# Two attention layers on one core: projections on 64-row tiles, weighted sums on four 32-column tiles, whole-array work gathered once per step

## The chip, the cores and the metric
The kernel runs on one core of a Trainium2 chip. The metric is the device time of one execution, in microseconds. The engines are named as the profile names them: PE is the matrix engine (TensorE), DVE the vector engine, ACT the scalar engine, POOL is GpSimd, SP issues the DMA transfers.

## The reference
Four layers run one after the other over 8 batches of 256 rows of 160 numbers, all in 32-bit floats: a narrow cross-attention with 20 heads of 8 (l0), a self-attention with 20 heads of 64 (a1), a cross-attention with 20 heads of 64 over a context of 512 rows of 256 (a2), and a gated feed-forward layer (ff). a1 and a2 are what the change rewrites:

```python
n = layer_norm(x, g, b)                       # x: 8 x 256 x 160
q = n @ wq                                    # wq: 160 x 1280, 20 heads of 64
k, v = src @ wk, src @ wv                     # a1: src = n; a2: src = context, 8 x 512 x 256
attn = softmax(q @ k.T / 8)                   # for each head
x = x + (attn @ v) @ wo + bo                  # heads joined to 1280; wo: 1280 x 160
```

## The kernel before
`attention_layer` (line 213) builds a1 and, with `cross` true, a2. Numbers that feed the softmax are split in a high part, rounded to the fast matmul type (fp32r), and a low part, the rest; a product is high by high, low by high and high by low. So a projection of n (160 rows) contracts 3 x 160 = 480 rows: `N_TERMS` (line 35) lays them out as three pieces of 128 rows and one of 96. The context's 256 rows give six pieces of 128 (`CTX_TERMS`, line 36).

The work goes in steps of two head pairs, that is four heads, 256 of the 1280 columns; 5 steps make a batch, 40 a layer. Each engine has its own program `step(d)`, unrolled over all steps, and the programs meet in semaphores. The steps are pipelined: step d projects for d, scores for d-1, computes the turned scores (keys on partitions) and exponentials for d-2, and the weighted sums for d-3 and d-2. A step has 2 slots in a1 and 4 in a2.

On PE (line 485), in this order: in each slot `score` (line 347, two heads side by side as 64-row tiles, for the row maxima), `turned_scores` (line 362, again 64-row tiles, 16 matmuls of 256 columns), then in some slots whole-array work, `keys` (402), `values` (418), `queries` (389), `output` (449) and the transposes `turn_max` (460), and in some the `weighted_sums` (432), which put the two heads of a pair in two 64-column tiles and are FP32: such a matmul is two instructions. The sums of the probabilities come from GpSimd's adds over the key tiles (`key_sums`, line 717, adds of 128x512) and a matmul with ones of 64 columns.

DVE takes the maxima (`maximum`, 620; one buffer `pscore`, so the next score waits for the last maximum), the low parts (`low_queries`, `low_keys`), reciprocal and product (`normalise`, 633), the layer norm (`dve_stats`, `dve_xhat`, `dve_n32`, lines 148 to 196) and adds the output. ACT takes the exponentials (`exp`, 535; one buffer `pst`), the high parts, the copy of the values and of the turned maxima. The queries, the keys and the values have a PSUM buffer each (`pa`, `pb`, `py`). The weights are split before the first step, on DVE and GpSimd (`Weights.low`, line 90).

## Time and profile before
| what | value |
|---|---|
| time, median of 3 runs | 1908.17 us (1907.72 to 1909.85) |
| the profiled execution: time, span | 1908.41 us, 1906.6 us |
| PE busy | 1742.8 us, 91% |
| DVE busy | 1325.7 us, 70% |
| ACT busy | 916.6 us, 48% |
| POOL busy | 443.8 us, 23% |
| mean granted clock of PE | 0.972 |
| HBM | 14 GB/s over the span |

The span runs from the first to the last instruction; the time has 1.8 us around it. Durations of matmuls overlap, since they are pipelined: what one costs is read from start to start. In a timeline row the columns are start, duration of the merged run, engine, line, operation, output and inputs, shape and count; in brackets stands how long the engine had been idle and who released it.

### The profile page before, as it was taken

What the parts mean: (1) busy time and instruction counts of PE and PEld (TensorE: products, weight loads), DVE (VectorE), ACT (ScalarE), POOL (GpSimd) and SP (SyncE); (2) the same over time, 40 slices, a digit from 0 to 9 for tenths busy, and PEclk for the clock granted to TensorE, in tenths of its full rate; (3) what the DMA queues carried; (4) which work ended last, traced back from release to release, by engine and by line L of the source; (5) the groups of instructions that cost most, each with busy time, mean ns of one, the idle gap of its engine ahead of it and who ended that gap; (6) DMA issues with size and microseconds to landing.
All of it is one profiled execution on the core that took longest, in us unless ns stands there. A gap on an engine that the chain in (4) does not pass through costs nothing. (4 is left out here: it accounts for less than half of the span.)

```text
span 1906.6 us, 36445 instructions
## 1 busy us (share of the span) xinstructions
PE 1742.8 (91%) x14528; PEld 1359.1 (71%) x14528; DVE 1325.7 (70%) x2210; ACT 916.6 (48%) x1636; POOL 443.8 (23%) x360
## 2 busy tenths in 40 slices
PE   5999989999959999999976999999999999999768
PEld 4667666666547777777755777777777777778568
DVE  5877877788668877888756666666656666665456
ACT  5878767778634343343323443434433434343223
POOL 1000000000022222222222443434343434343400
PEclk9999989999979999999987999999999999999979
DMA  6000000000030000000001000000000000000010
GB/s 195 17 18 1 18 19 18 1 18 1 1 101 1 1 2 1 2 1 2 1 7 37 12 1 13 1 12 1 12 1 12 1 12 1 1 2 1 1 44 21
DMA packets 11056, 29.23 MB, mean 15 GB/s; under 512 B 1872, under 2 KB 4944, under 8 KB 10896
## 3 DMA queue, kind: packets, MB, share of 16 engines
q1 hardware_dynamic: 10896, 26.94, 4.4%
q8 instruction: 119, 1.95, 0.4%
q14 instruction: 41, 0.34, 0.1%
HBM read 25.63 MB, written 1.31 MB: 14 GB/s over the span
## 5 line engine op out<-in xcount | busy, mean ns | idle before, releaser
L638 DVE RECIPROCAL a_recip<-a_pv 128x256 f32<-128x256 f32 x160 | 280.3, 1752 | 68.9 <-PE a_pv L446 68.2
L726 POOL TENSOR_TENSOR a_half_sum<-raw_weights 128x512 f32<-128x512 f32 x160 | 204.8, 1280 | 447.1 <-ACT raw_weights L541 447.1
L1101 DVE TENSOR_REDUCE l_negmax<-l_pscore 128x1 f32<-128x77 f32 (+1 forms) x640 | 233.2, 413 | 74.4 <-PE l_pscore L878 70.0
L541 ACT ACTIVATE raw_weights<-a_pst 128x1024 f32<-128x1024 f32 x160 | 164.1, 1026 | 246.3 <-PE a_pst L384 246.3
L627 DVE TENSOR_REDUCE a_negmax<-a_pscore 128x2 f32<-128x1024 f32 x160 | 195.5, 1222 | 97.1 <-PE a_pscore L358 96.1
L1018 ACT ACTIVATE l_probs<-l_pst 128x512 f32<-128x512 f32 x320 | 184.4, 598 | 75.3 <-PE l_pst L890 74.3
L541 ACT ACTIVATE a_probs<-a_pst 128x1024 f32<-128x1024 f32 x80 | 82.0, 1025 | 230.2 <-PE a_pst L384 230.2
L733 POOL TENSOR_TENSOR a_key_sum<-a_probs 128x512 f32<-128x512 f32 x80 | 102.1, 1276 | 309.8 <-ACT a_probs L541 309.8
L442 PE MATMUL a_pv<-raw_weights,a_v 128*64 128x256 f32 x1280 | 157.0, 388 | 2.6 <-DVE raw_weights L640 2.6
L878 PE MATMUL l_pscore<-l_k,l_qm 128*128 128x512 f32 x320 | 147.4, 461 | 11.5 <-DVE l_negmax L1101 6.0
L644 DVE TENSOR_TENSOR a_ql<-a_pa,a_qh 128x512 fp32r<-128x512 f32 x80 | 54.9, 686 | 146.2 <-ACT a_qh L547 146.1
L414 PE MATMUL a_pb<-a_ct,a_wk 128*128 128x512 f32 x480 | 133.9, 415 | 7.6 <-DVE a_ct L609 6.6
L375 PE MATMUL a_pst<-a_qh,a_kh 64*128 64x256 f32 x960 | 136.4, 280 | 3.7 <-ACT raw_weights L541 2.9
L381 PE MATMUL a_pst<-a_ql,a_kh 64*128 64x256 f32 x960 | 136.1, 279 | 0.0
L378 PE MATMUL a_pst<-a_qh,a_kl 64*128 64x256 f32 x960 | 135.8, 279 | 0.0
L384 PE MATMUL a_pst<-a_neg_t,a_sel 64*128 64x256 f32 x960 | 135.2, 278 | 0.0
L890 PE MATMUL l_pst<-l_qm,l_k 128*128 128x256 f32 x640 | 131.0, 287 | 4.0 <-ACT l_probs L1018 3.3
L428 PE MATMUL a_py<-a_wv,a_ct 128*128 128x256 f32 x960 | 131.6, 287 | 0.0
L890 PEld LDWEIGHTS l_pst<-l_qm,l_k 128*128 128x128 f32 x640 | 115.9, 192 | 21.7 <-issue 5.0
L428 PEld LDWEIGHTS a_py<-a_wv,a_ct 128*128 128x128 f32 x960 | 122.6, 190 | 8.9 <-issue 0.2
L145 POOL MEMSET a_ln_half<- 128x2 f32 x2 | 0.2, 99 | 546.0 <-POOLq L774 528.6
L358 PE MATMUL a_pscore<-a_kh,a_qh 64*128 64x256 f32 (+1 forms) x640 | 120.5, 414 | 4.6 <-DVE a_negmax L627 4.3
(156 smaller groups left out, 3534.9 us busy)
## 6 DMA issues: line engine op xcount, KB each, us to landing
l_ct<-in_ctx_t SPq DMA_DIRECT2D x8, 512.0 KB, 3.8
a_ct<-in_ctx_t SPq DMA_DIRECT2D x8, 512.0 KB, 3.6
l_x<-in_x_t SPq DMA_DIRECT2D x8, 256.0 KB, 2.8
raw_weights<-in_a_wk SPq DMA_DIRECT2D x3, 640.0 KB, 8.8
raw_weights<-in_a_wv SPq DMA_DIRECT2D x3, 640.0 KB, 10.9
a_wo<-in_a_wo SPq DMA_DIRECT2D x2, 800.0 KB, 5.2
xs<-in_x SPq DMA_DIRECT2D x8, 160.0 KB, 3.9
raw_weights<-in_a_wq SPq DMA_DIRECT2D x2, 640.0 KB, 5.1
```

Of the source, the lines that this page charges most:

```text
L375: mm(pst[:, h, j * SQ:(j + 1) * SQ], kh[own[h], buf, i, kt], qh[own[h], buf, i, :], start=True, stop=False)
L381: mm(pst[:, h, j * SQ:(j + 1) * SQ], kh[own[h], buf, i, kt], ql[own[h], buf, i, :], start=False, stop=False)
L428: last = mm(py[:, j * 256:(j + 1) * 256], acts[0:rows, xs_, kt * P:(kt + 1) * P], wv[0:rows, ws, 2 * u * P:2 * u * P + 256], start=k == 0, ...
L442: mm(pv[own[h], 0:SQ], v[:, kt, c0:c0 + D1], probs[:, par, h, kt, :], start=kt == 0, stop=kt == KT - 1)
L541: nc.scalar.activation(probs[:, g % 2, :, 2 * n:2 * n + 2, :], pst[:].rearrange("p h (k q) -> p h k q", k=2), ACT.Exp, scale=SCALE).then_i ...
L627: nc.vector.tensor_reduce(to, pscore[:], AX.X, ALU.max, negate=True).then_inc(max_done, 1)
L638: nc.vector.reciprocal(recip[:], pv[:, SQ:2 * SQ]).then_inc(recip_done, 1)
L726: nc.gpsimd.tensor_tensor(half_sum[:, n], probs[:, par, :, 2 * n, :], probs[:, par, :, 2 * n + 1, :], ALU.add).then_inc(half_done, 1)
L878: mm(pscore[:, i % 2, :], qm[:, buf, j, qt * P:(qt + 1) * P], k4[:, buf, :], start=True, stop=True).then_inc(score_ready, 1)
L890: last = mm(pst[:, n % 2, i * SQ:(i + 1) * SQ], k4[:, buf, kt * P:(kt + 1) * P], qm[:, buf, j, :], start=True, stop=True)
L1018: nc.scalar.activation(probs[:, par, j, 2 * kb:2 * kb + 2, :], pst[:, n % 2, :].rearrange("p (k q) -> p k q", k=2), ACT.Exp, scale=SCALE). ...
L1101: last = nc.vector.tensor_reduce(negmax[:, par, qt, j, s:s + 1], pscore[:, i % 2, keys], AX.X, ALU.max, negate=True)
```

## The change
`attention_layer` is replaced by `self_attention_layer` and `cross_attention_layer`, and the layer norm of both by `PairedNorm`.
- Queries and keys of n are projected on two 64-row tiles, one for each head pair. For that the normalised input is laid out with its 64-row halves doubled and its last 32 rows four times (12 pieces on DVE instead of 6, 6 transposes instead of 4, 3 gain steps of 256 instead of 2, splits of 768 elements), and eight pieces of 64 rows (`N_ROWS`) replace the four. The keys of the context go the same way (12 pieces of 64 rows for each pair, 512 columns wide). The values of a1 are on 64-row tiles too; those of a2 stay on the whole array.
- The weighted sums of both pairs of a step are made together, on four 32-column tiles, in two passes (x) for the two halves of a head's 64 numbers, and the ones have 32 columns. A step has one reciprocal and two products. Pairs and halves are ordered so on the host, in the weights.
- Order on PE: scores, turned scores and projections in the slots, then output, weighted sums, transposes and (a2) values once, at the step's end. The output of a batch is one block of 40 instructions.
- Queries, keys and values share one two-bank buffer, `pj`; the turned maxima are put in `pscore`, the turned norm in `pst`, the output in `px`, which also takes half of the weighted sums. In a2 the probabilities have one buffer and the context comes in three transfers a batch, doubled. GpSimd adds 128x1024 once a step in a1, and six times 128x512 in a2; its reciprocal root stands ahead of the key sums. The pipeline is one step shorter.

The core of the diff: the norm, then a1 (PE, DVE, GpSimd), then a2 (PE, DVE, GpSimd), where the removed lines are left out for a2.

```diff
+    def dve_xhat(self, dve, m):
+        nc = self.nc
+        dve.wait_ge(self.rstd_ready, m + 1)
+        for qt in range(QT):
+            scalars = (self.mv[:, qt, 0:1], self.rstd[:, qt:qt + 1])
+            for k in range(2):
+                nc.vector.tensor_scalar(self.xhat[:, qt, 0:2, k * D1:(k + 1) * D1],
+                                        self.xs[:, m, qt, 0:P].rearrange("p (c d) -> p c d", c=2),
+                                        *scalars, ALU.subtract, ALU.mult)
+            for k in range(4):
+                last = nc.vector.tensor_scalar(self.xhat[:, qt, 2, k * REST:(k + 1) * REST],
+                                               self.xs[:, m, qt, P:C], *scalars, ALU.subtract, ALU.mult)
+        last.then_inc(self.xhat_ready, 1)
+
+        dve.wait_ge(self.xhat_ready, m + 1)
+        nc.vector.tensor_tensor(self.xs[:, m], self.xs[:, m], self.rows, ALU.add).then_inc(self.biased, 1)
...
+    def pe_transpose(self, pe, m):
+        pe.wait_ge(self.xhat_ready, m + 1)
+        for g in range(3):
+            for qt in range(QT):
+                last = self.nc.tensor.transpose(self.turned(g)[:, qt * P:(qt + 1) * P], self.xhat[:, qt, g, :],
+                                                self.ident)
+        last.then_inc(self.t_ready, 1)
...
+
+
+
+N_ROWS = [(0, 0, 0), (1, 0, 1), (2, 0, 0), (3, 0, 1), (0, 1, 0), (1, 1, 1), (4, 0, 2), (4, 1, 2)]
+
+C_ROWS = [(0, 0, s) for s in range(4)] + [(1, 0, s) for s in range(4)] + [(0, 1, s) for s in range(4)]
+
+C_FULL = [(hw, hc, s) for hw, hc in ((0, 0), (1, 0), (0, 1)) for s in range(2)]
+OWN = [slice(h * D1, (h + 1) * D1) for h in range(2)]
+STEPS1 = PAIRS // 2
...
+            def queries_keys(d):
+                b, u = divmod(d, STEPS)
+                if u == 0:
+                    pe.wait_ge(ln.n_ready, b + 1)
+                wait(pe, v_copied, d)
+                for which, w in enumerate((wq, wk)):
+                    for k, (ws, hl, s) in enumerate(N_ROWS):
+                        for t in range(2):
+                            last = mm(pj[:, t, which * SQ:(which + 1) * SQ], w[OWN[t], ws, u * P:(u + 1) * P],
+                                      nts[b % 2][OWN[t], hl, s, :], start=k == 0, stop=k == len(N_ROWS) - 1)
+                last.then_inc(qk_ready, 1)
+
+            def values(d):
+                b, u = divmod(d, STEPS)
+                pe.wait_ge(qk_split, d + 1)
+                for k, (ws, hl, s) in enumerate(N_ROWS):
+                    for t in range(KT):
+                        last = mm(pj[:, t, 0:STEP_COLS], nts[b % 2][OWN[t], hl, s, t * P:(t + 1) * P],
+                                  wv[OWN[t], ws, u * STEP_COLS:(u + 1) * STEP_COLS],
+                                  start=k == 0, stop=k == len(N_ROWS) - 1)
+                last.then_inc(v_ready, 1)
+
+            def weighted_sums(e):
+
+                wait(pe, ot_ready, e)
+                pe.wait_ge(v_copied, e + 1)
+                pe.wait_ge(exp_done, 2 * e + 2)
+                if output_at(e + 3) is not None:
+                    pe.wait_ge(y_taken, output_at(e + 3) + 1)
+                for x in range(2):
+                    for kt in range(KT):
+                        for t in range(4):
+                            mm((pv, px)[x][t * 32:(t + 1) * 32, 0:SQ],
+                               v[:, e % RING, kt, t * D1 + x * 32:t * D1 + (x + 1) * 32], probs[:, e % 2, t, kt, :],
+                               start=kt == 0, stop=kt == KT - 1)
+                pe.wait_ge(sum_ready, e + 1)
+                for t in range(4):
+                    last = mm(pv[t * 32:(t + 1) * 32, SQ:2 * SQ], ones[:], key_sum[:, e % 2, t, :], start=True, stop=True)
...
+            def step(d):
+                for i in range(2):
+                    if here(d - 1):
+                        score(d - 1, i)
+                    if here(d - 2):
+                        turned_scores(d - 2, i)
+                    if i == 0 and here(d):
+                        queries_keys(d)
+                if output_at(d) is not None:
+                    output(output_at(d))
+                if here(d - 3):
+                    weighted_sums(d - 3)
+                if here(d - 1):
+                    turn_max(d - 1)
+                if next_norm(d, LN_TURN):
+                    turn_norm(d)
+                if here(d):
+                    if d == 0:
+                        pe.wait_ge(wv_done, 2)
+                    values(d)
+
+            ln.pe_transpose(pe, 0)
+            pe.wait_ge(ones_set, 1)
+            pe.wait_ge(wo_in, 16)
+            pe.wait_ge(wq_done, 1)
+            pe.wait_ge(wk_done, 1)
+            for d in range(LAST):
...
+                dve.wait_ge(qk_hi, d + 1)
+                subtract(qkl[:, d % RING], pj[:].rearrange("p i (w q) -> p i w q", w=2),
+                         qkh[:, d % RING].bitcast(FP32)).then_inc(qk_split, 1)
...
+            def step(d):
+                for i in range(2):
+                    if here(d - 1):
+                        maximum(d - 1, i)
+                if here(d):
+                    low_queries_keys(d)
+                if next_norm(d, LN_STATS):
+                    ln.dve_stats(dve, next_norm(d, LN_STATS))
+                if next_norm(d, LN_XHAT):
+                    ln.dve_xhat(dve, next_norm(d, LN_XHAT))
+                if next_norm(d, LN_TURN):
+                    ln.dve_n32(dve, next_norm(d, LN_TURN))
+                if next_norm(d, LN_SPLIT):
+                    b = next_norm(d, LN_SPLIT)
+                    ln.dve_lo(dve, b, nts[b % 2])
+                if output_at(d) is not None:
+                    add_output(output_at(d))
+                if here(d - 3):
...
+            def key_sums(e):
+
+                wait(pool, pv_done, e - 1)
+                pool.wait_ge(exp_done, 2 * e + 2)
+                nc.gpsimd.tensor_tensor(key_sum[:, e % 2], probs[:, e % 2, :, 0, :], probs[:, e % 2, :, 1, :],
+                                        ALU.add).then_inc(sum_ready, 1)
...
+                wait(pe, v_copied, d)
+                for k, (ws, hl, s) in enumerate(N_ROWS):
+                    for t in range(2):
+                        last = mm(pj[:, t, 0:SQ], wq[OWN[t], ws, u * P:(u + 1) * P], nt[OWN[t], hl, s, :],
+                                  start=k == 0, stop=k == len(N_ROWS) - 1)
...
+            def keys(d, part):
                 b, u = divmod(d, STEPS)
+                if part == 0:
+                    if u == 0:
+                        pe.wait_ge(c_ready, b + 1)
+                    pe.wait_ge(q_split, d + 1)
+                half = len(C_ROWS) // 2
+                for k in range(part * half, (part + 1) * half):
+                    hw, hc, s = C_ROWS[k]
+                    for t in range(2):
+                        last = mm(pj[:, t, :], wk[OWN[t], hw, s, u * P:(u + 1) * P], cts[b % 2][OWN[t], hc, s, :],
+                                  start=k == 0, stop=k == len(C_ROWS) - 1)
+                if part == 1:
+                    last.then_inc(k_ready, 1)
+
+            def values(d):
                 b, u = divmod(d, STEPS)
+                pe.wait_ge(k_split, d + 1)
+                for kt in range(KT):
+                    for k, (hw, hc, s) in enumerate(C_FULL):
+                        last = mm(pj[:, kt // 2, (kt % 2) * STEP_COLS:(kt % 2 + 1) * STEP_COLS],
+                                  cts[b % 2][:, hc, 2 * s, kt * P:(kt + 1) * P],
+                                  wv[:, hw, s, u * STEP_COLS:(u + 1) * STEP_COLS],
+                                  start=k == 0, stop=k == len(C_FULL) - 1)
                 last.then_inc(v_ready, 1)
...
+            def weighted_sums(e):
+
+                wait(pe, ot_ready, e)
+                pe.wait_ge(v_copied, e + 1)
+                for n in range(2):
+                    pe.wait_ge(exp_done, SLOTS * e + 2 * n + 2)
+                    for x in range(2):
+                        if n == 0 and x == 1 and output_at(e + 2) is not None:
+                            pe.wait_ge(y_taken, output_at(e + 2) + 1)
+                        for kt in (2 * n, 2 * n + 1):
+                            for t in range(4):
+                                mm((pv, px)[x][t * 32:(t + 1) * 32, 0:SQ],
+                                   v[:, e % 2, kt, t * D1 + x * 32:t * D1 + (x + 1) * 32], probs[:, t, kt, :],
+                                   start=kt == 0, stop=kt == KT - 1)
+                pe.wait_ge(sum_ready, 2 * e + 2)
+                for t in range(4):
+                    last = mm(pv[t * 32:(t + 1) * 32, SQ:2 * SQ], ones[:], key_sum[:, t, :], start=True, stop=True)
...
+                    if here(d) and s == 0:
+                        queries(d)
+                    if here(d) and s in (1, 2):
+                        if d == 0 and s == 1:
+                            pe.wait_ge(wk_done, 1)
+                        keys(d, s - 1)
+                if output_at(d) is not None:
+                    output(output_at(d))
+                if here(d - 2):
+                    weighted_sums(d - 2)
+                if here(d - 1):
+                    turn_max(d - 1)
+                if next_norm(d, LN_TURN):
+                    turn_norm(d)
+                if here(d):
+                    if d == 0:
+                        pe.wait_ge(wv_done, 1)
+                    values(d)
+            pe.wait_ge(wq_done, 1)
...
             def step(d):
                 for s in range(SLOTS):
                     if here(d - 1):
                         maximum(d - 1, s)
+                    if s == 0:
+                        if here(d):
                             low_queries(d)
+                        if next_norm(d, LN_SPLIT):
+                            ln.dve_lo(dve, next_norm(d, LN_SPLIT), nt)
+                    if s == 1 and next_norm(d, LN_STATS):
+                        ln.dve_stats(dve, next_norm(d, LN_STATS))
+                    if s == 1 and next_norm(d, LN_XHAT):
+                        ln.dve_xhat(dve, next_norm(d, LN_XHAT))
+                    if s == 2 and next_norm(d, CTX_SPLIT):
+                        low_context(next_norm(d, CTX_SPLIT))
+                if output_at(d) is not None:
+                    add_output(output_at(d))
+                if here(d):
+                    low_keys(d)
+                if next_norm(d, LN_TURN):
...
+            def key_sums(e):
+
+                add = nc.gpsimd.tensor_tensor
+                wait(pool, pv_done, e)
+                for i in range(2):
+                    two = slice(2 * i, 2 * i + 2)
                     pool.wait_ge(exp_done, SLOTS * e + i + 1)
+                    add(key_sum[:, two], probs[:, two, 0, :], probs[:, two, 1, :], ALU.add).then_inc(part_sum, 1)
+                for i in range(2):
+                    two = slice(2 * i, 2 * i + 2)
+                    pool.wait_ge(part_sum, 4 * e + 2 + i)
+                    pool.wait_ge(exp_done, SLOTS * e + i + 3)
+                    add(key_sum[:, two], key_sum[:, two], probs[:, two, 2, :], ALU.add).then_inc(part_sum, 1)
+                    pool.wait_ge(part_sum, 4 * e + 3 + i)
+                    add(key_sum[:, two], key_sum[:, two], probs[:, two, 3, :], ALU.add).then_inc(sum_ready, 1)
 
             ln.pool_setup(pool)
...
+                if next_norm(d, LN_STATS):
                     ln.pool_rstd(pool, next_norm(d, LN_STATS))
+                if here(d - 2):
+                    key_sums(d - 2)
```

## Rows read from the trace of the kernel before
**Rows 1.** Busy by window, self and cross: length, PE, PEld, DVE, ACT, POOL; clock, DMA.
```profile
556.53:964.00 407.47, 399.80 (x3751) 318.62 (x3750) 330.63 (x436) 164.48 (x247) 101.90 (x83) 1.00 0.02 7
1025.39:1771.58 746.19, 727.59 (x6347) 573.73 (x6347) 472.99 (x562) 297.65 (x408) 296.43 (x235) 1.00 0.02 5
```

**Rows 2.** PE timeline of a cross step (instructions of weight loads left out).
```profile
1422.06 1.66 PE L414 MATMUL a_pb<-a_ct,a_wk 128*128 128x512 f32 x6
1423.56 1.58 PE L428 MATMUL a_py<-a_wv,a_ct 128*128 128x256 f32 x12
1425.07 0.50 PE L358 MATMUL a_pscore<-a_kh,a_qh 64*128 64x512 f32 x2
1425.41 0.28 PE L375 MATMUL a_pst<-a_qh,a_kh 64*128 64x256 f32 x2
...
1426.24 0.28 PE L384 MATMUL a_pst<-a_neg_t,a_sel 64*128 64x256 f32 x2
1426.45 1.95 PE L442 MATMUL a_pv<-raw_weights,a_v 128*64 128x256 f32 x16
1428.23 0.60 PE L446 MATMUL a_pv<-a_key_sum,a_ones 128*64 128x256 f32 x4
1428.76 1.21 PE L398 MATMUL a_pa<-a_nt,a_wq 128*128 128x256 f32 x8
...
1435.76 2.88 PE L456 MATMUL a_py<-a_wo,raw_weights 128*128 128x160 f32 x20
```

**Rows 3.** PE timeline: first scores of two neighbouring self and cross steps.
```profile
696.93 0.39 PE L358 MATMUL a_pscore<-a_kh,a_qh 64*128 64x256 f32 x2
...
706.31 0.39 PE L358 MATMUL a_pscore<-a_kh,a_qh 64*128 64x256 f32 x2
...
1384.21 0.49 PE L358 MATMUL a_pscore<-a_kh,a_qh 64*128 64x512 f32 x2
...
1401.97 0.50 PE L358 MATMUL a_pscore<-a_kh,a_qh 64*128 64x512 f32 x2
```

**Rows 4.** PE timeline in the first layer, four 32-column tiles, and the next instruction.
```profile
301.25 0.64 PE L938 MATMUL l_pv<-l_probs,l_v 128*32 128x256 f32 x8
301.81 0.48 PE L972 MATMUL l_pd<-l_sums,l_pick 128*128 128x256 f32 x1
```

**Rows 5.** Groups by form: busy us, mean ns, idle before and its releaser.
```profile
L638 DVE RECIPROCAL a_recip<-a_pv 128x256 f32<-128x256 f32 x160 | 280.3, 1752 | 68.9 <-PE a_pv L446 68.2
...
L627 DVE TENSOR_REDUCE a_negmax<-a_pscore 128x2 f32<-128x1024 f32 x160 | 195.5, 1222 | 97.1 <-PE a_pscore L358 96.1
...
L644 DVE TENSOR_TENSOR a_ql<-a_pa,a_qh 128x512 fp32r<-128x512 f32 x80 | 54.9, 686 | 146.2 <-ACT a_qh L547 146.1
...
L640 DVE TENSOR_TENSOR raw_weights<-a_pv,a_recip 128x256 f32<-128x256 f32 x80 | 34.0, 424 | 2.7
...
L541 ACT ACTIVATE raw_weights<-a_pst 128x1024 f32<-128x1024 f32 x160 | 164.1, 1026 | 246.3 <-PE a_pst L384 246.3
...
L547 ACT ACTIVATE a_qh<-a_pa 128x512 fp32r<-128x512 f32 x80 | 47.8, 598 | 95.6 <-PE a_pa L398 93.1
```

**Rows 6.** DVE and GpSimd timeline at the norm: a self, then a cross step.
```profile
714.61 0.50 DVE L173 TENSOR_SCALAR a_ln_xhat<-xs,a_ln_mv,a_ln_rstd 128x32 f32<-128x32 f32 x2
715.02 0.36 DVE L171 TENSOR_SCALAR a_ln_xhat<-xs,a_ln_mv,a_ln_rstd 128x160 f32<-128x160 f32 x1
...
715.83 0.49 DVE L178 TENSOR_TENSOR xs<-xs,a_bo_rows 128x320 f32<-128x320 f32 x1
...
1533.23 1.57 DVE L173 TENSOR_SCALAR a_ln_xhat<-xs,a_ln_mv,a_ln_rstd 128x32 f32<-128x32 f32 x2
...
1533.25 1.30 POOL L726 TENSOR_TENSOR a_half_sum<-raw_weights 128x512 f32<-128x512 f32 x1 [1.56 <-ACT raw_weights L541]
...
1534.84 1.44 DVE L178 TENSOR_TENSOR xs<-xs,a_bo_rows 128x320 f32<-128x320 f32 x1
```

**Rows 7.** PE timeline: the first keys of the cross layer.
```profile
1016.33 1.19 PE L414 MATMUL a_pb<-a_ct,a_wk 128*128 128x512 f32 x2 [6.63 <-DVE a_ct L609]
```

826 lines of the change are left out of this document (460 added, 366 removed).

## The prediction
> **What bounds the kernel now.** The shares of the page (the table above) name the matrix engine (PE), but they are a mean over four layers, of which the diff leaves the first and the last alone. So I asked the busy times by stage, from the first score matmul of each rewritten layer to the first of its last step: PE is busy 98% of 407 us in self-attention and 97.5% of 746 us in cross-attention, at full clock, with the vector engine (DVE) at 81% and 63% [rows 1]. So both layers are PE-bound, and the order of PE's own work sets the pace. The PE timeline shows what a step consists of [rows 2]. The reader is to look at start-to-start distances there, since durations overlap: a regular self step is 706.31 - 696.93 = 9.38 us, a cross step 1401.97 - 1384.21 = 17.76 us [rows 3].
>
> **What the edits are worth on PE.** Start-to-start prices [rows 2]: a pair of 64-row matmuls of 256 columns 0.118 us (1425.41 to 1426.24 is seven), a whole-array matmul of 256 columns the same 0.118 (12 between 1423.56 and 1425.07, less the change of shape), of 512 columns 0.23 (six in 1.50, less the change), and two 64-column FP32 instructions side by side 0.216 (eight such groups 1426.45 to 1428.23, less 0.05).
> - Projections. Before, two pairs' queries take 8 whole-array matmuls (four row pieces, the last with 96 rows); after, 8 pairs of 64-row matmuls: 0.94 us each way. The same holds for the self keys and values. Cross keys: 12 of 512 columns against 12 pairs, 2.8 us each way (only single pairs of 512 are shown; they lie between 0.216 and 0.23, at most 0.2 us a step). So the tiling itself gives nothing.
> - Weighted sums. Four 32-column tiles replace two 64-column ones, over twice the passes: 8 groups of 0.216 in self, 16 in cross, as before. Only the sums with ones halve, from 4 groups to 2: -0.43 us a step. Four tiles abreast are seen in the first layer: 8 instructions in 0.56 us with a change of shape in it, so two groups of about 0.22 [rows 4].
> - Changes of shape. Between two kinds of tiles the next start is late by about 0.1 us, and the first item costs 0.1 more: 1425.07 to 1425.41 is 0.34 for a pair worth 0.23, and 1428.23 to 1428.76 is 0.53 for two groups of 0.216. I take 0.20 for a change, 0.13 for one into the column tiles. Before, a self step has 6 and a cross step 10; after, each has 3 (4 with the output). That is -0.5 and -1.3 us.
> - The max transposes, the output (20 instructions in 2.72 us, so 5.44 a batch [rows 2]), scores and turned scores cost the same.
>
> Self step: two slots of 0.235 + 0.94, 1.88 for queries and keys, 0.09 + 1.78 + 0.53 weighted, 0.37 turn, 1.05 values = 8.05. Nothing late is longer: DVE has two maxima of 1.22, one split of 1024 (0.686 for 512 and 0.424 for 256 elements give 1.21), one reciprocal of 1.75 instead of two, two products of 0.42, in all about 6.3 us [rows 5]. -1.33 us a step.
>
> Cross step: PE's sum is 15.95, but two chains now end later. The projections share one buffer, so keys wait until the queries are out. A hand-over from PE takes the 0.28 us of the last matmul and up to 0.1 more. The first turned scores end at 1.43 us after the step's start, the exponential (1.03) at 2.5, then come the high part on the scalar engine (ACT, 0.6) and the low part on DVE (0.69) [rows 5]: keys start at 3.83, where PE was ready at about 3.4. With that the last exponential ends at 10.15; GpSimd then has two chained adds of 1.3 for the second pair [rows 6], so the sums stand at 12.95 where PE is ready at 12.5. Ones, turn and values end at 16.93. -0.83 us a step.
> Over the 39 steps between first and last score: -52 us and -32 us.
>
> **What the special steps take back.** A batch has steps with norm, output or splits. Before, they cost 407.5 - 39 x 9.38 = 41.7 us in self, plus 4.4 by which the first steps are short, so 46; in cross 53.6 + 7.5 = 61 [rows 1, 3]. After, for each of seven batches:
> - The normalised input. Its 6 pieces and the bias add become 12 and the add, 3.1 us of DVE at the 0.21 us from piece to piece of the smaller ones (two between 714.61 and 715.02), some more for the larger. DVE instructions that read and write SBUF alone wait out a GpSimd add: two pieces worth 0.50 took 1.57 and an add worth 0.49 took 1.44 while GpSimd was adding [rows 6]. In cross, max 1 ends at 4.9, and what is queued behind the pieces is max 2, for which score 3 waits. Free of GpSimd, score 3 starts at 9.2 instead of 7.7: 1.5 us. With GpSimd's adds at 5.0 to 6.2 and 7.8 to 10.3 it is 12.8: 5.1. I take 4.7, near the upper end, since the rows show the blocking. In self the one add of 1024 (2.6 us) starts just ahead of the pieces; the normalisation and then the next step's first max are queued behind: 1.9 to 4.0, taken 3.8.
> - The output in one block: 5.64 each, in self 0.7 more until the sum in the shared bank is taken. In cross that block covers the 0.4 us wait of the sums.
> - The transposed norm: 6 transposes instead of 4, 1.05 us; in self its three gain steps (0.45 apart) stand ahead of the normalisation and cost another 1.4.
> - Cross alone: the split of the norm delays max 1 by 0.9; and GpSimd's reciprocal root stands ahead of the key sums in its queue, waits for the statistics that follow max 1 on DVE (6.0), and six adds of 1.3 then end at 14.6: 1.65. The context split (2048 elements, 2.3 us of DVE, 2 of ACT) and its three loads lie beside the output.
> Sum: self 7 x (3.8 + 2.4 + 6.4) = 88, cross 7 x (9.9 + 1.05 + 0.9 + 1.65) = 94.5. Against before: +42 and +33.5, and +2.4 because the first steps, already short, save less.
>
> **Ends of the layers.** DVE splits more at the start, and GpSimd's split of 2560 elements (about 6 us at the rate of its adds) holds DVE up. In self the first projection stays where it was, but queries, split and values then follow one another: first score +3. In cross the keys start at about 1022 instead of 1016.3 [rows 7] and values wait for their split: first score +7.6. The pipeline is one step shorter, and a drained step has one reciprocal: -4.6 and -4.3. Net +1.7.
>
> **Sum.** -52 - 32 + 42 + 33.5 + 2.4 + 1.7 = -4.4 us. The profiled execution took 1908.4 us with a span of 1906.6, 0.2 above the median of 1908.2; so **1904 us**. 0.2%, about what a measurement of this kernel can tell from no change, is 4 us.
>
> **Rivals.**
> - **DVE is not held up** (faster). If the norm's pieces slip between GpSimd's adds, the stalls fall to 1.5 and 1.9: -22 - 13, 1868 us. For it: the same pieces in a self step run free, the add in 0.49 [rows 6]. Against it: this time GpSimd's adds are timed onto them by the exponentials.
> - **Four abreast does not stream** (slower). Four tiles need a weight load and a matmul every 54 ns; the fastest long stream in the trace, the paired 64-row matmuls, has one per 59 ns [rows 2], and the first layer shows four abreast only in bursts of 8 [rows 4]. At 59 the group takes 0.235: 19 ns x 28 groups (10 in a self step, 18 in a cross step) x 40 = +21 us, 1925. It turns the sign from some 7 ns a group on (+8 us). The Trainium skill (TensorE: Matmul & The Clock Gate, "Wait — 56ns, not 53.3ns?") says that with hardware decode off the sequencer spends about 62 ns on a matmul; by that a group would take 0.248 and the estimate would be +36 us, 1940. The burst neither shows nor excludes it, since its eight may have been waiting ready in the engine; the paired stream at 59 speaks a little against 62.
> - **Two abreast.** If the passes of four tiles ran as two pairs, the same 28 groups would double: 28 x 0.216 x 40 = +242 us, 2146. The burst of 8 in 0.56 us speaks against it [rows 4].
>
> **How the numbers follow.** The forecast has 0.50, with its own range 1886 to 1922 (0.15 us a self step and 0.3 a cross step either way, and a part of the stalls' bounds); of that 0.24 is faster, 0.16 same, 0.10 slower. DVE free 0.23 (0.22 faster, 0.01 same), the stream's limit 0.22 (slower), two abreast 0.05 (slower). Faster 0.46, same 0.17, slower 0.37. The range of 1868 to 1935 leaves out the lower half of the free case and the upper part of the limited one with the last.
>
> **What would show it.** Right: self steps of about 8.05 and cross steps of about 16.9 us; a cross step with three changes of shape, keys waiting 0.4 us for the query split; 5 us before score 3 in the third step of a batch, behind DVE pieces that last over 1 us; the ones matmuls waiting for GpSimd. Wrong: groups of four further apart than 0.22 us; PE idle in regular steps by more than 1 us; or no idle time at the norm.

## The result, and the profile after

The changed kernel took **1927.8 us**, the median of 4 runs (1925.9 to 1928.2), beside 1909.0 us for the kernel before (4 runs): a ratio of 1.0102, with a 95% interval of 1.0088 to 1.0116. It is 1% **slower**. The forecast was 1904, slightly faster; the range held the time, the direction was wrong. The profiled execution took 1925.9 us with a span of 1924.1.

First the stages, as for [rows 1]: the busy times of the profile after in two windows, from the first score of self-attention to the first of its last step, and the same in cross-attention.

```profile
560.91:966.03 405.12, 371.76 (x5284) 309.84 (x5282) 297.22 (x388) 161.47 (x200) 94.64 (x45) 0.96 0.02 8
1033.60:1792.10 758.50, 702.29 (x8379) 563.69 (x8378) 438.89 (x523) 284.15 (x322) 296.05 (x235) 0.98 0.04 10
```

Self-attention became 2.4 us shorter (407.5 to 405.1), cross-attention 12.3 us longer (746.2 to 758.5), and what lies outside the two windows 7.6 us longer (752.9 to 760.5 of the spans). The reader is to see two things. PE is busy for only 92 and 93% of the stages, after 98 and 97.5%: there are waits now. And the granted clock, 1.00 in both stages before, is 0.96 and 0.98. The clock is a mean; somewhere inside PE ran slow.

A regular step did become faster, by as much as forecast. The PE timeline of the profile after, first scores of two neighbouring self steps and of two cross steps, against [rows 3]:

```profile
857.42 0.41 PE L437 MATMUL a_pscore<-a_qkh 64*128 64x256 f32 x4
...
865.50 0.28 PE L437 MATMUL a_pscore<-a_qkh 64*128 64x256 f32 x2
...
1503.26 0.50 PE L801 MATMUL a_pscore<-a_kh,a_qh 64*128 64x512 f32 x2
...
1520.43 0.50 PE L801 MATMUL a_pscore<-a_kh,a_qh 64*128 64x512 f32 x2
```

That is 8.08 us for 9.38 in self and 17.17 for 17.76 in cross (forecast 8.05 and 16.93). So the loss is in the special steps. The list of waits of the profile after, for PE (total, times, longest), says which:

```profile
PE a_pscore L801 <- DVE a_negmax L1016: 33.4, 15, 4.2
PE a_pscore L437 <- DVE a_negmax L609: 24.2, 14, 3.4
...
PE a_pv L882 <- POOL raw_weights L1098: 18.7, 31, 1.7
```

The first two are scores that wait for a row maximum: six long waits of 3.38 us in self and seven of 4.20 in cross, one to a batch. The third are the sums with ones, which wait for GpSimd's adds (0.34 us in a regular step, 1.65 in the second step of a batch). This is one of them, the timeline of the third step of a cross batch, which starts at 1439.62 (DVE, PE and GpSimd; POOL is GpSimd):

```profile
1444.46 1.58 DVE L280 TENSOR_SCALAR a_ln_xhat<-xs,a_ln_mv,a_ln_rstd 128x128 f32<-128x128 f32 x2
1444.62 1.34 POOL L1091 TENSOR_TENSOR raw_weights<-raw_weights 128x512 f32<-128x512 f32 x1 [0.98 <-ACT raw_weights L951]
...
1445.97 0.91 DVE L284 TENSOR_SCALAR a_ln_xhat<-xs,a_ln_mv,a_ln_rstd 128x32 f32<-128x32 f32 x4
...
1446.16 1.56 PE L850 MATMUL a_pj<-a_ct,a_wk 64*128 64x512 f32 x12
...
1447.31 2.90 DVE L284 TENSOR_SCALAR a_ln_xhat<-xs,a_ln_mv,a_ln_rstd 128x32 f32<-128x32 f32 x4
1447.54 1.26 POOL L1096 TENSOR_TENSOR raw_weights<-raw_weights 128x512 f32<-128x512 f32 x1 [1.58 <-ACT raw_weights L951]
1448.88 1.29 POOL L1098 TENSOR_TENSOR raw_weights<-raw_weights 128x512 f32<-128x512 f32 x1
1450.24 0.49 DVE L289 TENSOR_TENSOR xs<-xs,a_bo_rows 128x320 f32<-128x320 f32 x1
1450.65 1.22 DVE L1016 TENSOR_REDUCE a_negmax<-a_pscore 128x2 f32<-128x1024 f32 x1
...
1451.92 0.50 PE L801 MATMUL a_pscore<-a_kh,a_qh 64*128 64x512 f32 x2 [4.20 <-DVE a_negmax L1016]
...
1452.84 0.42 PE L826 MATMUL a_pst<-a_neg_t,a_sel 64*128 64x256 f32 x2
```

Four small pieces of the norm take 0.91 us when GpSimd is idle and 2.90 while it adds. Behind them stands the maximum (L1016), and for that PE waits 4.20 us before the fourth score of the step (the prediction counts from 0 and calls it score 3). Then look at the pairs of turned scores behind the wait: they last 0.42 us each, while in a regular step of the same kernel a pair lasts 0.28. Windows of the same step show why (columns as in [rows 1]; the last but two is the clock):

```profile
1439.62:1447.70 8.08, 8.08 (x95) 6.61 (x94) 6.20 (x13) 6.39 (x6) 2.79 (x3) 1.00 0.01 2
1447.70:1452.30 4.60, 0.40 (x6) 0.34 (x6) 4.57 (x6) 0.00 (x0) 2.39 (x2) 1.00 0.00 0
1452.30:1455.70 3.40, 3.40 (x24) 3.18 (x21) 2.90 (x2) 1.55 (x2) 0.39 (x1) 0.50 0.09 13
1455.70:1467.75 12.05, 12.05 (x134) 9.96 (x132) 4.13 (x5) 0.77 (x2) 2.14 (x2) 1.00 0.32 85
```

PE is idle for over four of the 4.60 us of the second window, and in the third, busy throughout, its clock is 0.50: 1.2 GHz instead of 2.4. The step takes 28.1 us; less half of those 3.40 it would be 26.4 (an estimate).

### The profile page after: what moved, and what is told of

Its sections match the earlier page's. It is cut to its first block and busy times, and to the rows that moved or that the text cites. A ratio compares the mean times of both kernels' runs of the same rounds, so it can differ in the third digit from the quotient of the medians.

```text
span 1924.1 us, 42997 instructions
## 1 busy us (share of the span) xinstructions
PE 1687.0 (88%) x18240; PEld 1338.9 (70%) x18240; DVE 1256.3 (65%) x2134; ACT 901.8 (47%) x1498; POOL 436.0 (23%) x318
## 5 line engine op out<-in xcount | busy, mean ns | idle before, releaser
L1016 DVE TENSOR_REDUCE a_negmax<-a_pscore 128x2 f32<-128x1024 f32 x160 | 195.6, 1222 | 108.2 <-PE a_pscore L801 108.2
L1091 POOL TENSOR_TENSOR raw_weights<-raw_weights 128x512 f32<-128x512 f32 x80 | 103.2, 1293 | 305.1 <-ACT raw_weights L951 305.1
L679 POOL TENSOR_TENSOR a_key_sum<-a_probs 128x1024 f32<-128x1024 f32 x40 | 94.8, 2370 | 278.8 <-ACT a_probs L560 278.8
L850 PE MATMUL a_pj<-a_ct,a_wk 64*128 64x512 f32 x960 | 130.8, 405 | 7.1 <-DVE a_ql L1004 6.7
L860 PE MATMUL a_pj<-a_wv,a_ct 128*128 128x256 f32 x960 | 126.3, 287 | 3.2 <-DVE a_kl L1004 3.2
L1096 POOL TENSOR_TENSOR raw_weights<-raw_weights 128x512 f32<-128x512 f32 x80 | 102.6, 1283 | 99.0 <-ACT raw_weights L951 98.6
L609 DVE TENSOR_REDUCE a_negmax<-a_pscore 128x4 f32<-128x1024 f32 x80 | 97.7, 1221 | 41.3 <-PE a_pscore L437 41.3
L1030 DVE RECIPROCAL a_recip<-a_pv 128x256 f32<-128x256 f32 x40 | 70.2, 1756 | 80.3 <-PE a_pv L882 80.3
L860 PEld LDWEIGHTS a_pj<-a_wv,a_ct 128*128 128x128 f32 x960 | 119.0, 191 | 3.8 <-issue 2.9
L850 PEld LDWEIGHTS a_pj<-a_ct,a_wk 64*128 64x128 f32 x960 | 88.4, 188 | 28.1 <-DVE a_ql L1004 7.8
L1098 POOL TENSOR_TENSOR raw_weights<-raw_weights 128x512 f32<-128x512 f32 x80 | 102.3, 1279 | 6.3
L1300 PE MATMUL l_pv<-l_probs,l_v 128*32 128x256 f32 x1280 | 102.9, 394 | 0.5 <-ACT l_sums L1423 0.5
L801 PE MATMUL a_pscore<-a_kh,a_qh 64*128 64x512 f32 x320 | 71.7, 440 | 33.4 <-DVE a_negmax L1016 33.4
```

The lines of the kernel that those rows point to most:

```text
L850: last = mm(pj[:, t, :], wk[OWN[t], hw, s, u * P:(u + 1) * P], cts[b % 2][OWN[t], hc, s, :], start=k == 0, stop=k == len(C_ROWS) - 1)
L860: last = mm(pj[:, kt // 2, (kt % 2) * STEP_COLS:(kt % 2 + 1) * STEP_COLS], cts[b % 2][:, hc, 2 * s, kt * P:(kt + 1) * P], wv[:, hw, s, u * ...
L1016: nc.vector.tensor_reduce(to, pscore[:], AX.X, ALU.max, negate=True).then_inc(max_done, 1)
L1091: add(key_sum[:, two], probs[:, two, 0, :], probs[:, two, 1, :], ALU.add).then_inc(part_sum, 1)
L1096: add(key_sum[:, two], key_sum[:, two], probs[:, two, 2, :], ALU.add).then_inc(part_sum, 1)
L1098: add(key_sum[:, two], key_sum[:, two], probs[:, two, 3, :], ALU.add).then_inc(sum_ready, 1)
```

## The experiments

All are the changed kernel with a small edit; times are medians, each with its ratio to the kernel before on the same chip.

| run | time, us | ratio to before [95%] |
|---|---|---|
| the change itself | 1927.8 | 1.0102 [1.0088, 1.0116] |
| key sums wait for the norm | 1877.6 | 0.9842 [0.9825, 0.9859] |
| cross pieces behind the last maximum | 1896.3 | 0.9942 [0.992, 0.9965] |
| cross key sums ahead of the root | 1922.7 | 1.0078 [1.006, 1.0095] |
| self pieces one batch earlier | 1900.4 | 0.9958 [0.9944, 0.9972] |
| 80 whole-array extras | 1949.7 | 1.0199 [1.0174, 1.0225] |
| 80 row-tile extras | 1933.6 | 1.0127 [1.0107, 1.0147] |
| filling in the cross wait | 1916.9 | 1.0036 [1.0014, 1.0057] |
| filling in self, a step too early | 1947.8 | 1.0228 [1.0203, 1.0253] |
| filling in self, at the wait | 1950.8 | 1.023 [1.0213, 1.0247] |
| three orders together | 1861.5 | 0.9747 [0.9726, 0.9769] |
| and the output taken later | 1860.9 | 0.977 [0.9752, 0.9788] |
| and the pieces after the keys | 1851.0 | 0.9711 [0.9691, 0.9731] |

**1. Are the norm's pieces on DVE and GpSimd's adds what collides?** GpSimd's key sums are held back, in both layers, until the pieces and the bias add are through. The work is the same, only GpSimd's starts later.

```
+                if next_norm(d, LN_XHAT):
+                    pool.wait_ge(ln.biased, next_norm(d, LN_XHAT) + 1)
                 if here(d - 2):
                     key_sums(d - 2)
```

> GpSimd's key sums wait, in the step with the norm, until DVE has finished the norm's pieces; DVE's work and order are unchanged. Blocking theory (the pieces last long because they wait out GpSimd's adds, and PE's clock is halved after the long wait): in cross PE's wait before score 3 falls from 4.2 us to about 1.3, in self from 3.4 to about 1.7, the half-speed stretches behind them go, and seven batches give back 32 us and 20 us: about 1876 us, 1895 if the clock still falls. Rival (the number of pieces costs, not the blocking): waits stay above 3.5 and 3 us, time within 4 us of 1928.

Measured: 1877.6 us, 50 us less than the change and 1.6% less than before. The timeline of a third cross step (it starts at 1499.40):

```profile
1504.24 0.59 DVE L280 TENSOR_SCALAR a_ln_xhat<-xs,a_ln_mv,a_ln_rstd 128x128 f32<-128x128 f32 x2
1504.75 0.91 DVE L284 TENSOR_SCALAR a_ln_xhat<-xs,a_ln_mv,a_ln_rstd 128x32 f32<-128x32 f32 x4
1505.58 0.60 DVE L280 TENSOR_SCALAR a_ln_xhat<-xs,a_ln_mv,a_ln_rstd 128x128 f32<-128x128 f32 x2
1506.09 0.91 DVE L284 TENSOR_SCALAR a_ln_xhat<-xs,a_ln_mv,a_ln_rstd 128x32 f32<-128x32 f32 x4
...
1508.72 0.50 PE L803 MATMUL a_pscore<-a_kh,a_qh 64*128 64x512 f32 x2 [1.23 <-DVE a_negmax L1018]
```

Each set of four is now 0.91 and PE's wait is 1.23 us instead of 4.20. The third step fell from 28.1 to 23.6 in cross and from about 14.0 to 10.4 in self. In both the saving exceeds what came off the wait (3.0 in cross; in self 3.38 to 1.42, so 2.0): the rest is the clock, which no longer falls behind that wait. In the 5 us behind the self wait it is 1.00 in all six batches, where the change had 0.50, 0.66 or, once, 1.00. The collision is shown. DVE's share of the two stages, 73 and 58% after 81 and 63 before, would not have told of it.

**2. The same in cross by order alone.** The pieces leave the place between two maxima and go behind the step's last maximum, ahead of the output's sum and the keys' low part.

```
-                    if s == 1 and next_norm(d, LN_XHAT):
-                        ln.dve_xhat(dve, next_norm(d, LN_XHAT))
...
+                if next_norm(d, LN_XHAT):
+                    ln.dve_xhat(dve, next_norm(d, LN_XHAT))
                 if output_at(d) is not None:
                     add_output(output_at(d))
```

> Cross layer alone: the norm's pieces are moved behind the last maximum of the step, where PE has 5.4 us of output matmuls. Theory (it is the queue place on DVE, max 2 behind the pieces, that stops PE): the third step of a batch falls from 28.1 us to about 22.3, its half-speed stretch goes, seven batches give 41 us: about 1887 us. Rival (the pieces hurt wherever they stand, since the output's sum and the key split queue behind them): the step stays above 26 us, gain under 15 us.

Measured: 1896.3 us; the third step takes 23.3, not 22.3. The DVE timeline shows what was left out of the estimate:

```profile
1530.22 1.55 DVE L280 TENSOR_SCALAR a_ln_xhat<-xs,a_ln_mv,a_ln_rstd 128x128 f32<-128x128 f32 x2
1531.69 2.84 DVE L284 TENSOR_SCALAR a_ln_xhat<-xs,a_ln_mv,a_ln_rstd 128x32 f32<-128x32 f32 x4
```

The pieces are still stretched by GpSimd's adds, only no maximum stands behind them now; the output's sum does, for which PE waits 1.0 us. With some 5 us less in each of those steps the stage falls from 758.5 to 728.3 us.

**3. The reciprocal root on GpSimd**, which stands ahead of the key sums in the second cross step: the two are swapped.

```
-                if next_norm(d, LN_STATS):
-                    ln.pool_rstd(pool, next_norm(d, LN_STATS))
                 if here(d - 2):
                     key_sums(d - 2)
+                if next_norm(d, LN_STATS):
+                    ln.pool_rstd(pool, next_norm(d, LN_STATS))
```

> Cross layer alone: GpSimd's reciprocal root stands behind the key sums of its step instead of ahead. Theory: the second step of a batch, 18.3 us, falls to the 17.1 of a regular one, seven times 1.2: -8 us, about 1920. Rival (that step is long for the statistics on DVE, not for the queue): 18.3 stays, 1928.

Measured: 1922.7 us. The second step went from 18.33 to 17.01 us, as priced, 7.9 us in six batches. The whole gained only 5, since the third steps took 28.1 to 29.2 us, 28.87 on average, where they had taken 28.45. The pieces and the wait did not move. In the timeline of the third step that starts at 1434.59,

```profile
1439.43 1.58 DVE L280 TENSOR_SCALAR a_ln_xhat<-xs,a_ln_mv,a_ln_rstd 128x128 f32<-128x128 f32 x2
...
1446.88 0.80 PE L801 MATMUL a_pscore<-a_kh,a_qh 64*128 64x512 f32 x2 [4.20 <-DVE a_negmax L1016]
```

the pieces begin 4.84 us into the step and the fourth score comes at 12.29, as in the change (4.84 and 12.30). What differs is the clock behind the wait: 0.50 over the 3.40 us from that score, and 0.77 over the next 4.7, where the same 3.40 us of the change's step at 1439.62 had 0.56 and the stretch from 1455.70 to 1458.00 already 0.99. Why the clock stays low for longer no run shows. It does so in the change too: its third steps take 28.0 to 29.5 us with the same wait of 4.20 in each.

**4. The same in self**, where the statistics and the pieces of a batch are made one batch earlier, under the output's 40 matmuls (two helpers give the new steps; GpSimd's root moves along).

```
-                if next_norm(d, LN_STATS):
-                    ln.dve_stats(dve, next_norm(d, LN_STATS))
-                if next_norm(d, LN_XHAT):
-                    ln.dve_xhat(dve, next_norm(d, LN_XHAT))
+                if d == 1:
+                    ln.dve_xhat(dve, 1)
...
                 if output_at(d) is not None:
                     add_output(output_at(d))
+                if norm_stats(d):
+                    ln.dve_stats(dve, norm_stats(d))
+                if d != 1 and norm_xhat(d):
+                    ln.dve_xhat(dve, norm_xhat(d))
                 if here(d - 3):
                     normalise(d - 3)
```

> Self layer alone: the norm's pieces of a batch are made one batch earlier, in the output step behind the add of the output. Theory: the third step of a batch falls from 14.0 us by the 3.4 us wait and what the half clock adds, to about 9.5, the output step grows by 0.3: about -4.2 us in six batches, 1903 us. Rival (DVE is too full in self for the pieces anywhere, since its regular step has 6.3 us of 8.07): the stall moves to the step behind the output, gain under 8 us.

Measured: 1900.4 us. The third self step takes 8.72 instead of 12.4 to 14.9, the stage 377.1 us instead of 405.1, and cross is unchanged. The move has a price, paid once: in the first batch no output's matmuls cover the pieces, PE waits 4.31 us for a maximum behind them, and that step takes 14.93 us instead of 9.43.

**5. What a change of shape costs.** One extra matmul of 128 columns ahead of the third and the fourth score of every cross step, over the whole array or on one row tile (the score that follows overwrites its result; the last line is that of the second run):

```
+                if s in (2, 3):
+                    if e == 0:
+                        pe.wait_ge(sel_set, 2)
+                    mm(pscore[:, 0, 0:P], sel[:, 0, :], sel[:, 1, :], start=True, stop=True)
...
+                    mm(pscore[:, 0, 0:P], sel[OWN[0], 0, :], sel[OWN[0], 1, :], start=True, stop=True)
```

> One extra matmul of 128 columns over the whole array ahead of the third and the fourth score of every cross step (80 in all), among 64-row work on both sides, so that each brings two changes of shape. By the price that the prediction took (0.20 us for a change) a step grows by 2 x (0.06 + 0.40) = 0.9 us, 80 x 0.46 = 37 us in all, less what is hidden in the steps where TensorE waits for the third score anyway: 1927.8 + 34 = about 1962 us, and about 30 us over the run with the 64-row extra. If changes of shape cost nothing, this run and that one agree within 2 us. If they cost twice what was taken, the difference is 60.

> The same 80 extra matmuls of 128 columns at the same places, but each on one 64-row tile, like its neighbours: no change of shape. 80 x 0.06 = 5 us over the changed kernel, 1933 us, in every theory; it is the reference for the run with the whole-array extra.

Measured: 1949.7 and 1933.6 us. In the PE timeline of the first, two extras and the step around them:

```profile
1413.42 0.51 PE L805 MATMUL a_pscore<-a_kh,a_qh 64*128 64x512 f32 x2
...
1419.01 0.33 PE L803 MATMUL a_pscore<-a_sel 128*128 128x128 f32 x1
...
1422.05 0.33 PE L803 MATMUL a_pscore<-a_sel 128*128 128x128 f32 x1
...
1431.48 0.50 PE L805 MATMUL a_pscore<-a_kh,a_qh 64*128 64x512 f32 x2
```

and in that of the second, the same step:

```profile
1407.24 0.50 PE L805 MATMUL a_pscore<-a_kh,a_qh 64*128 64x512 f32 x2
...
1424.56 0.50 PE L805 MATMUL a_pscore<-a_kh,a_qh 64*128 64x512 f32 x2
```

18.06 against 17.32 us: 0.74 for four changes, 0.185 each, where 0.20 was taken. Yet the whole differs by 16 us and not by 30. The price is right, the count was not: in the second step of a batch both kernels take 18.3, since there the key sums are late and hide it, and in the third PE waits anyway. The difference was paid in about three steps of five.

**6. What the half clock costs.** PE gets work for the time of its cross wait: 16 matmuls of 512 columns whose result nothing reads. The kernel's computation is as before.

```
+                    if s == 2 and next_norm(d, LN_XHAT) and here(d - 3):
+                        pe.wait_ge(ot_ready, d - 2)
+                        for _ in range(16):
+                            mm(px[:, :], sel[OWN[0], 0, :], kh[OWN[0], (d - 1) % 2, 0, :], start=True, stop=True)
```

> In the third step of each later cross batch TensorE gets 16 matmuls of 64 rows and 512 columns, whose result nothing reads, for the 4.2 us in which it waits for the third score's maximum. The wait itself cannot become shorter by this. If the half clock behind that wait is what costs 1.2 to 1.7 us a batch, the granted clock stays at 1.00 there, the step goes from 28.1 to about 26.6 and the whole to about 1917 us (7 batches). If the low clock costs nothing, because something else than TensorE is late there, the time stays at 1928 or grows by the 16 matmuls where they outlast the wait.

Measured: 1916.9 us, 11 less than the change. The windows of the third step that starts at 1530.39; the third part begins at the fourth score:

```profile
1530.39:1538.34 7.95, 7.95 (x95) 6.79 (x95) 6.06 (x13) 6.40 (x6) 2.65 (x3) 1.00 0.00 0
1538.34:1542.76 4.42, 3.80 (x18) 2.76 (x16) 4.39 (x7) 0.00 (x0) 2.58 (x2) 1.00 0.00 0
1542.76:1546.16 3.40, 3.40 (x33) 3.21 (x34) 3.28 (x2) 1.90 (x2) 0.73 (x1) 1.00 0.02 5
1546.16:1557.05 10.89, 10.89 (x127) 8.80 (x126) 4.14 (x5) 0.42 (x2) 1.81 (x2) 1.00 0.44 99
```

The fourth score starts 12.4 us into the step, as without the filling (12.3): the wait is untouched. But the clock stays at 1.00 behind it, 33 matmuls start in the 3.40 us from that score, where the same 3.40 us of the change (1451.92 to 1455.32) had 23 and a clock of 0.56, and the step takes 26.65 us, in each of the six batches that were filled, where it took 28.0 to 29.5, 28.45 on average. **A kernel with 16 more matmuls to a batch is faster**, since PE's idle time costs twice: once as a wait and once, at half clock, behind it. Six times 1.80 is 10.8 us, and the whole became 11 shorter.

The same was tried in self-attention.

> The same in self-attention: in the third step of each later batch TensorE gets 16 matmuls of 64 rows and 512 columns, whose result nothing reads, for the 3.4 us in which it waits for the second score's maximum. If the half clock behind the wait costs 1.6 to 2.5 us a batch (five of those steps took 13.9 to 14.9 us and one, without it, 12.4), the seven third steps all take 12.4 to 12.6 us, and the whole becomes 1927.8 - 11 = about 1917 us. If the low clock costs nothing, or if the filling outlasts the wait, those steps stay at 13.9 or more and the time at 1928 or above.

Measured: 1947.8 us. The filling stood a step too early: the second steps went from 8.07 to 11.70 us, six times 3.63, and the waiting steps were unchanged. This miss is a useful control: where PE does not wait, 16 such matmuls cost 3.6 us. One step later:

> The filling one step later, where the self-attention wait is (in the run before it stood a step too early, where TensorE has no wait, and cost its full 3.6 us six times: 1947.8 us). The 16 matmuls lie now in the 3.4 us of the wait for the second score's maximum. If the half clock behind the wait costs 1.6 to 2.5 us a batch, the seven third steps all take 12.4 to 12.8 us and the whole 1927.8 - 11 = about 1917 us; if it costs nothing, 1928 or more.

Measured: 1950.8 us, with third steps of 18.0 (one of 16.5). The filling writes a bank that DVE reads last in its normalisation, and this is itself queued behind the norm's pieces:

```profile
621.50 4.61 PE L533 MATMUL a_px<-a_qkh,a_sel 64*128 64x512 f32 x14 [2.25 <-DVE a_ot L628]
```

So PE waited 2.25 us before it could begin to fill, and the clock fell to 0.50 all the same. The experiment didn't isolate the self layer's clock. For that the first experiment speaks, which took 3.6 us off a self step and 2.0 off its wait, and the trace of the change. Two third steps of its self-attention, the one whose clock held and one of the others:

```profile
829.41:841.80 12.39, 9.01 (x140) 7.40 (x138) 9.80 (x22) 4.07 (x5) 2.37 (x1) 1.00 0.01 1
881.65:895.61 13.96, 10.58 (x142) 8.01 (x139) 9.79 (x22) 4.06 (x5) 2.36 (x1) 0.88 0.00 1
```

DVE has 9.80 and 9.79 us of work in both, and PE idles 3.4 in both; with the lower clock PE's same work takes 1.57 us more. The six steps of this kind took 12.4 to 14.9.

**7. A version that beats both.** The moves of experiments 2, 3 and 4 together:

> Three moves of order together: in self-attention the normalised input one batch earlier, under the output's matmuls; in cross-attention the norm's pieces behind the step's splits, and the key sums ahead of the reciprocal root on GpSimd. If they act on different waits and add up, 1927.8 - 27.5 - 31.5 - 5 = 1864 us; cross steps: first of a batch 17.2, second 17.0, third 23.3. If the key sums ahead of the root delay the statistics' result and so the pieces (which now come late in the step anyway), the gain of the third move is lost as it was alone: 1869 us or more.

Measured: 1861.5 us. The gains add up: 66 us together, 64 as the sum of the three alone. The second step takes 17.04 us, as in experiment 3, and the third stays at 23.3. Two more moves on top of it. First PE's wait for the output's sum in self:

```
-                if output_at(e + 3) is not None:
-                    pe.wait_ge(y_taken, output_at(e + 3) + 1)
                 for x in range(2):
+                    if x == 1 and output_at(e + 3) is not None:
+                        pe.wait_ge(y_taken, output_at(e + 3) + 1)
```

> The three moves of order, and in self-attention TensorE waits for the output's sum in the shared bank only before the second half of the weighted sums, the half that writes to this bank. The 0.67 us of that wait is then covered by 16 matmuls of the first half (0.86 us): 8 x 0.67 = 5.4 us less, 1861.5 - 5 = 1856 us, self steps with an output 14.95. If the wait is not what is late there but the reciprocal behind it, the step stays at 15.62 and the time at 1861.5.

Measured: 1860.9, nothing gained. The output step fell from 15.62 to 14.89 as expected, and the next one rose from 8.10 to 8.83. In that stretch DVE works without a break from the output's sum to the next maxima; the reciprocal and the first maximum are late whether PE arrives early or not. Then the pieces in cross, behind the sum and the keys' low part:

```
-                if next_norm(d, LN_XHAT):
-                    ln.dve_xhat(dve, next_norm(d, LN_XHAT))
                 if output_at(d) is not None:
                     add_output(output_at(d))
                 if here(d):
                     low_keys(d)
+                if next_norm(d, LN_XHAT):
+                    ln.dve_xhat(dve, next_norm(d, LN_XHAT))
```

> As the last, and in cross-attention the norm's pieces stand behind the output's sum and the keys' low part instead of ahead of them. TensorE no longer waits 1.0 us for that sum, seven times: 1856 - 7 = 1849 us, third steps 22.3. But the pieces (3.5 us once GpSimd has ended) then stand ahead of the reciprocal, which comes 1.2 us later, and with it the next step's first maximum: if that is what TensorE then waits for, the fourth step of a batch takes 18.5 instead of 17.7 and the sum is 1855 us.

Measured: **1851.0 us**, 2.9% less than before and about 4% less than the change. Third steps take 22.12 us and the fourth 17.68, the better of the two cases; by then GpSimd's adds are over and the pieces take 0.59 and 0.92 us a set. The expectation counted 7 us for seven such steps; the cross stage became 12 us shorter, since the third step of the first batch, which has no output to cover the pieces, fell from 23.05 to 18.13 as well.

## Why the prediction was wrong

**Regular steps: right in self, nearly so in cross.** -1.30 us a self step where -1.33 was forecast, -0.6 to -0.7 a cross step where -0.83 was. Over the 39 steps of a stage this is 51 us (forecast 52) and 23 to 28 (forecast 32). In cross the sums with ones start 13.35 us into a regular step, where 12.95 was worked out. The argument behind it held: sixteen matmuls on row tiles still take 0.94 us from start to start (two such blocks of a self step start at 830.60 and 831.54), so the tiles gain nothing, and a change of shape costs 0.185 us where 0.20 was taken. No run isolates what the halved sums with ones give.

**The stream of four tiles: the rival is dead.** The PE timeline of the profile after:

```profile
1430.50 1.07 PE L877 MATMUL a_pv<-raw_weights,a_v 128*32 128x256 f32 x16
1431.39 1.05 PE L877 MATMUL a_px<-raw_weights,a_v 128*32 128x256 f32 x16
1432.25 1.05 PE L877 MATMUL a_pv<-raw_weights,a_v 128*32 128x256 f32 x16
1433.12 1.05 PE L877 MATMUL a_px<-raw_weights,a_v 128*32 128x256 f32 x16
1435.82 0.64 PE L882 MATMUL a_pv<-raw_weights,a_ones 128*32 128x256 f32 x8 [1.65 <-POOL raw_weights L1098]
```

Sixteen start every 0.86 to 0.89 us, 54 to 56 ns each, for 64 in a row: 0.22 a group, where 0.216 was taken. The rival's 59 ns would have made 0.94 of it, so both it and the pairing of tiles are excluded. The Trainium skill (TensorE: Matmul & The Clock Gate, "Wait — 56ns, not 53.3ns?") gives about 62 ns for a matmul with hardware decode off. That bound did not hold here; whether hardware decode was off, no run shows. So the slower result is not this rival's, though its 1925 us lies close to the measured time.

**The special steps: the term that failed.** The place, the cause and the length of the stall were right. In the third cross step score 3, the fourth, was put 12.8 us into the step if GpSimd stands in the way, 4.7 was taken for the delay, and it came at 12.3, 4.6 late. In self 3.8 was taken, and 4.3 is what the step shows at full clock (12.39 - 8.07). What the working priced at nothing was **PE's clock behind the stall**. Six third cross steps took 28.0 to 29.5 us, and 26.65 with the wait filled: 10.8 us, shown by experiment 6. In self five third steps took 1.5 to 2.6 us more than the one whose clock held, 9.8 us in all; this is read from the trace. Together 20.6 us, where the profiled span grew by 17.5: without them the change would have come out about 3 us below the kernel before (an estimate from these figures).

Other terms were off as well, and by luck they nearly cancel. In cross the forecast took 16.93 + 9.9 = 26.8 for the third step, near the 26.65 at full clock. The stage's excess of 9.6 over the forecast (758.5 against 746.2 - 32 + 33.5 and some 1.2 for the first steps) is the clock's 10.8, plus 9.4 because a regular step takes 17.17 and not 16.93, less about 10 because the other special steps cost less: the second 1.16 us more than a regular one where 1.65 was taken, the fourth and the fifth together 1.17 where 1.95 was, and the third 0.4 less than taken. In self the sum of the special steps came out at 88.7 us against 88: the clock's 9.8 and 3 more of stall stand against 10 by which the output and the turned norm cost less (the step of both takes 7.55 more than a regular one instead of 8.8) and 2.4 of the first batch, which has hardly a stall.

**Starts and ends: under-priced, for a cause that stays open.** Outside the two windows +1.7 was forecast and +7.6 measured: 4.4 up to the first self score (3 was taken), 6.2 between the layers (3.0), and -3.0 behind the last cross step (-4.3). In self the first four steps were taken to be short; they took 8.75, 8.33, 8.70 and 9.43 us (the last has a norm in it), all above the regular 8.07. Windows of the profile after just behind the first score, then of before:

```profile
560.90:567.40 6.50, 4.64 (x46) 3.99 (x42) 3.04 (x3) 1.68 (x3) 0.56 (x1) 0.74 0.88 375
567.40:571.00 3.60, 3.00 (x30) 3.00 (x32) 3.57 (x14) 0.93 (x2) 0.00 (x0) 0.62 0.02 5
```

```profile
556.50:563.40 6.90, 6.13 (x53) 5.22 (x54) 5.98 (x16) 2.67 (x5) 0.69 (x1) 0.95 0.84 332
563.40:570.00 6.60, 6.60 (x66) 5.69 (x64) 4.79 (x7) 4.41 (x8) 2.57 (x2) 1.00 0.01 2
```

Before, PE was busy and at full clock there; after, queries, split and values follow one another with gaps, and the clock is 0.62 to 0.74. The clock explains little of it. In the run with the cross wait filled, whose self layer is the same program, the stretch from 567.40 to 571.00 had a clock of 1.00, and the first two steps took 7.35 and 7.73 us instead of 8.75 and 8.33; but the first score came 1.2 us later, and the fourth step began at 585.97 instead of 586.69, 0.7 earlier. Even so the four steps took 33.3 us, where the forecast had them below four regular ones (32.3).

**The sum.** In the profiled spans the forecast is short by 22 us: about 10 in cross, 6 in self (most of it in the first four steps), 6 outside. The sign turned on this, since gains of 84 us and losses of 80 stood against each other and 4.4 was left. Without the 20.6 us of the clock it would have been short by about 1. Of the rivals, a DVE that is not held up was put at 1868. The change did not behave so (four pieces took 2.90 us); when GpSimd's sums were made to wait, which brings that state about, the time was 1877.6.

## What to carry to other kernels

When a merge of small steps lets one engine do more per instruction, look at what else the longer step lines up: here twelve small pieces of a norm fell under another engine's adds, and the maximum that the bottleneck needed stood behind them. Price a long idle gap of the matrix engine twice (here 3.4 and 4.2 us; gaps of 1.2 to 1.7 us cost only themselves), as the wait and as the stretch at half clock behind it, and read the granted clock of the stretch after each long wait. Before giving a merge up, try the order: moving the same instructions behind the ones that somebody waits for turned a loss of 1.0% into a gain of 2.9%.

## What was not expected of the hardware

- **The clock behind a wait.** After 4.20 us without work PE ran the next 3.40 us at 0.50 to 0.56 in the steps looked at. After the 3.38 us waits in self the clock was 0.50 to 0.66 over the next 5 us five times out of six, and 1.00 once; behind the 1.23 and 1.42 us waits of the first experiment it was 1.00. The Trainium skill (TensorE: Matmul & The Clock Gate, "HAM oscillation — how this bites in real kernels") describes a kernel that goes cold behind every wait in its loop; the trace agrees, with 0.50 in the window behind the wait, though here the wait is for DVE and the page's is for a DMA. The prediction should have weighed it.
- **The blocking goes both ways.** DVE's small pieces wait out GpSimd's adds (0.91 against 2.90 us for four). And an add on GpSimd waits out a DVE subtraction that reads two operands in SBUF. The timeline of the version with three orders:

```profile
1400.15 2.28 DVE L1017 TENSOR_TENSOR a_ct<-a_ct 128x2048 fp32r<-128x2048 f32 x1
1401.14 2.42 POOL L1109 TENSOR_TENSOR raw_weights<-raw_weights 128x512 f32<-128x512 f32 x1 [1.63 <-ACT raw_weights L964]
1402.35 1.22 DVE L1029 TENSOR_REDUCE a_negmax<-a_pscore 128x2 f32<-128x1024 f32 x1
...
1403.64 1.31 POOL L1111 TENSOR_TENSOR raw_weights<-raw_weights 128x512 f32<-128x512 f32 x1
```

  The add takes 2.42 us where its neighbours of the same size take 1.3; the maximum, which reads another memory (PSUM), is not held up (1.22). The Trainium skill (SBUF — State Buffer, "SBUF: two separate sides") has it that DVE and GpSimd share one pair of ports, which a GpSimd operation and a DVE operation in a two-port mode or with two SBUF inputs take as an exclusive lock, and whoever starts first keeps it for its whole instruction. The row agrees: the subtraction ends at 1402.43 (1400.15 + 2.28), and the add, which began inside it, ends 1.13 us after that. In which mode the norm's pieces run, no run shows.
- **A matmul on one row tile between others of its kind is nearly free** (0.07 us for 128 columns: two of them make a step 17.32 instead of 17.17), while the same matmul over the whole array costs 0.44 (18.06).
